# A decoder layer in one kernel: order of the expert's splits and scaling, column tiles for the gate product, a later wait for a low part

## What is computed

```python
# 1 attention, 16 heads of 32, chunks of 128 tokens
q, k, v = silu(x @ Wq), silu(x @ Wk), x @ Wv        # q, k rotated
o = lightning_attention(q, k, v)                    # decayed scores in a chunk, a state between chunks
o = rmsnorm_per_head(o * sigmoid(x @ Wg1 @ Wg2)) * norm_weight
x = layernorm(x + o @ Wo)                           # Wg1 is 512x32, Wg2 is 32x512
# 2 four experts chosen by token id, weights ctx
x = layernorm(x + expert_by_token_id(x))
# 3 48 experts, top 8 of each token, at most 192 tokens for an expert
g, u = split(xb[e] @ gate_up[e].T)                  # 192x512 @ 512x384
y[e] = (silu(g) * u) @ down[e].T                    # 192x192 @ 192x512
x = layernorm(x + sum of y, weighted)
```

## Time and profile before

| | |
|---|---|
| median of 3 runs | 951.74 us (949.85 to 955.11) |
| profiled execution, its own time | 962.05 us |
| span from first to last instruction | 960.2 us |
| PE busy | 856.5 us (89%) |
| DVE, ACT, POOL busy | 637.9, 397.1, 473.4 us |
| mean granted TensorE clock | 0.961 |

### The profile page before, as it was taken

How to read it: one execution, slowest core, us unless ns; L and a number is a source line. 1 busy time by engine, 2 the same in 40 slices (tenths; PEclk the granted TensorE clock), 3 DMA queues, 4 the chain that set the end, 5 groups by cost and what they waited for, 6 DMA issues and landing times. The chain is left out here.

```text
span 960.2 us, 18373 instructions
## 1 busy us (share of the span) xinstructions
PE 856.5 (89%) x5878; PEld 729.9 (76%) x5879; DVE 637.9 (66%) x1454; ACT 397.1 (41%) x805; POOL 473.4 (49%) x443
## 2 busy tenths in 40 slices
PE   6899999999999889999998699999999999999700
PEld 4787788778887668888887498888888888888600
DVE  6767765676567556777777667676776667666426
ACT  4333233222332412233322046666666665666504
POOL 0242333233433322555555357777776777775344
PEclk9899999999999999999999899999999999999955
DMA  9541112111210035322222849999999999997665
GB/s 331 189 167 45 45 45 87 44 44 44 86 45 33 23 109 167 105 101 99 94 93 99 288 127 287 265 274 280 268 271 268 280 275 261 287 236 164 164 168 215
DMA packets 72461, 155.39 MB, mean 162 GB/s; under 512 B 9872, under 2 KB 10304, under 8 KB 72032
## 3 DMA queue, kind: packets, MB, share of 16 engines
q1 hardware_dynamic: 49840, 99.40, 31.5%
q0 software_dynamic: 22576, 55.42, 23.8%
HBM read 110.27 MB, written 44.52 MB: 161 GB/s over the span
## 5 line engine op out<-in xcount | busy, mean ns | idle before, releaser
L1884 POOL DMA_INDIRECT y_rows<-arena,place_token x96 | 154.9, 1614 | 91.1 <-issue 72.0
L1873 POOL DMA_INDIRECT xg<-x_rows,place_token x96 | 103.5, 1078 | 43.0 <-issue 26.8
L940 PE MATMUL ps<-arena,raw 128*128 128x192 f32 x576 | 100.9, 333 | 1.2 <-DVE arena L1662 0.9
L940 PEld LDWEIGHTS ps<-arena,raw 128*128 128x128 f32 x576 | 95.9, 194 | 4.9 <-issue 4.2
L589 PE MATMUL ps<-w_hi,x_hi 128*128 128x512 f32 (+1 forms) x332 | 79.2, 361 | 4.6 <-DVE x_lo L1396 3.8
L940 PE MATMUL ps<-arena,mid_flat 128*128 128x192 f32 x432 | 74.7, 330 | 2.3 <-DVE arena L1662 2.3
L940 PEld LDWEIGHTS ps<-arena,mid_flat 128*128 128x128 f32 x432 | 69.9, 190 | 8.8 <-DVE arena L1662 8.5
L589 PE MATMUL ps<-w_lo,x_hi 128*128 128x512 f32 (+1 forms) x332 | 74.3, 346 | 0.0
L589 PE MATMUL ps<-w_hi,x_lo 128*128 128x512 f32 (+1 forms) x332 | 74.2, 346 | 0.0
L1745 POOL TENSOR_TENSOR arena<-arena,attn_pack 128x512 f32<-128x512 f32 x12 | 16.8, 1403 | 116.0 <-DVE arena L1287 116.0
L1146 ACT ACTIVATE arena<-ps,arena 96x512 f32<-96x512 f32 x48 | 32.8, 683 | 97.7 <-PE ps L953 94.8
(11 more groups left out here) (231 smaller groups left out, 1971.7 us busy)
## 6 DMA issues: line engine op xcount, KB each, us to landing
raw<-in_gu SPq DMA_DIRECT2D x24, 768.0 KB
mid_flat<-in_gu SPq DMA_DIRECT2D x18, 768.0 KB
raw<-in_dn SPq DMA_DIRECT2D x24, 256.0 KB
y_rows<-zero SPq DMA_DIRECT2D x20, 256.0 KB
mid_flat<-in_dn SPq DMA_DIRECT2D x18, 256.0 KB
arena<-in_gu SPq DMA_DIRECT2D x6, 768.0 KB
arena<-in_xT SPq DMA_DIRECT2D x16, 256.0 KB
x_res<-in_x SPq DMA_DIRECT2D x16, 256.0 KB, 2.7
```

What stands on the lines that cost most here:

```text
L940: m = pe.matmul(out, wgu[slot][:, q, part * P:(part + 1) * P], xgT[:, p, q, :], start=(q == 0), stop=(q == KC - 1))
L1873: pool.indirect_dma_start(out=xg[:, place, h, :], out_offset=None, in_=x2_d, in_offset=bass.IndirectOffsetOnAxis(ap=place_token[:, 2 * n + ...
L1884: pool.indirect_dma_start(out=y2_d if p and n < DUAL else y_d, out_offset=bass.IndirectOffsetOnAxis(ap=place_token[:, 2 * n + h:2 * n + h ...
```

## The change

Stage A: Wg1 is held once; `gate_low` becomes four separate products, one for each k, whose results lie in four column positions (partitions 0 to 31, 32 to 63 and so on), not summed. ACT's copy of them is plain float32 with 128 rows, and `gate_high` is four float32 products over 128 rows with Wg2 stacked four times, which does the sum. `low_g1`, `wg2_parts` and their two preparing instructions go. `project_o` starts on `o_high` and waits for the low part at its third pass. On DVE `low_o` moves behind the cut of the state's addition.

Stage C: on ACT the split of n's down weights comes first in turn n and `scale_y(n-1)` last; on DVE likewise: down weights' low part, h, `copy_x`, h's low part, `scale_y(n-1)`, `keep_w`. Scatter 42 no longer waits for scatter 41.

```diff
@@ ATTN_PACK
-             ("dq", P, (G, P)), ("block", P, (P,)), ("wg1", P, (KC, 3 * RANK))]
+             ("dq", P, (G, P)), ("block", P, (P,)), ("wg1", P, (KC, RANK))]
@@ tensor: gate_low, project_o, gate_high
-                    m = pe.matmul(ps[0:3 * RANK, PM, 0:P], wg1[:, k, :], xT[:, c % 2, k, :], start=(k == 0), stop=(k == KC - 1))
+                    m = pe.matmul(ps[k * RANK:(k + 1) * RANK, PM, 0:P], wg1[:, k, :], xT[:, c % 2, k, :], start=True, stop=True, skip_group_check=True)
...
-                pe.wait_ge(oT_copied, t + 1)
+                pe.wait_ge(o_high, t + 1)
...
-                three_passes(ps[:, PM, :], o_hi, o_lo, w_hi[:, 3], w_lo[:, 3], between=between).then_inc(wo_made, 1)
+                three_passes(ps[:, PM, :], o_hi, o_lo, w_hi[:, 3], w_lo[:, 3], (oT_copied, t + 1), between).then_inc(wo_made, 1)
...
-                pe.wait_ge(g1_low, t + 1)
+                pe.wait_ge(g1_copied, t + 1)
                 for g in range(G):
-                    m = pe.matmul(ps[:, PM, g * P:(g + 1) * P], wg2_parts[:, g * P:(g + 1) * P], g1_parts[:, :], start=True, stop=True)
+                    m = pe.matmul(ps[:, PM, g * P:(g + 1) * P], wg2[:, g * P:(g + 1) * P], g1[:, :], start=True, stop=True)
@@ scalar: c_expert
+                act.wait_ge(*weights_of(slot, turn))
+                at_least(act, dn_made[p], k)
+                act.activation(wdn_hi[p][:, 0, :], wdn[slot], ACT.Copy)
+                act.activation(wdn_hi[p][0:P // 2, 1, :], wdn_rest[slot], ACT.Copy)
+                act.activation(wdn_hi[p][P // 2:P, 1, :], wdn_rest[slot], ACT.Copy).then_inc(dn_high, 1)
                 act.wait_ge(gu_made[p], k + 1)
...
                 if not last:
                     copy_x(1 - p, k + p)
-                if not first:
-                    scale_y(1 - p, k - (1 - p))
-
-                act.wait_ge(*weights_of(slot, turn))
...
                 act.activation(hc_hi[P // 2:P, p, :], h_c[P // 2:P, p, :], ACT.Copy).then_inc(h_high, 1)
+                if not first:
+                    scale_y(1 - p, k - (1 - p))
@@ vector: a_tile
                 mask(t)
-                if not first:
-                    low_o(*last_of(b, c))
                 if c < CH - 1:
...
                                       block_diag[:, :].unsqueeze(1).to_broadcast([P, G, P]), ALU.mult).then_inc(add_cut, 1)
+                if not first:
+                    low_o(*last_of(b, c))
+                if c < CH - 1:
                     dve.wait_ge(add_cut, n + 1)
@@ vector: c_expert
+                dve.wait_ge(dn_high, 2 * k + p + 1)
+                dve.tensor_tensor(wdn_lo[p][:, 0, :], wdn[slot], wdn_hi[p][:, 0, :].bitcast(F32), ALU.subtract)
+                dve.tensor_tensor(wdn_lo[p][LO, 1, :], wdn_rest[slot], wdn_hi[p][rest_rows[slot], 1, :].bitcast(F32), ALU.subtract)\
+                   .then_inc(dn_split[p], 1)
                 dve.wait_ge(g_made, 2 * (2 * k + p) + 1)
...
                 if not last:
                     copy_x(1 - p, k + p)
+                dve.wait_ge(h_high, 2 * k + p + 1)
+                dve.tensor_tensor(ha_lo[:, p, :], h_a[:, p, :], ha_hi[:, p, :].bitcast(F32), ALU.subtract)
+                dve.tensor_tensor(hc[HI, p, :], h_c[HI, p, :], hc_hi[HI, p, :].bitcast(F32), ALU.subtract).then_inc(h_split, 1)
                 if not first:
                     scale_y(1 - p, k - (1 - p))
...
@@ gpsimd: c_scatter
-                if n >= DUAL:
+                if n > DUAL:
                     pool.wait_ge(y_added[1 - p], 32 * (k + p))
```

More of the change, by code:

```diff
@@ L205, in build @@
         weighted = take("weighted", [P, H, P])
-        wg2 = take("wg2", [3 * RANK, D]); wg2_parts = sb("wg2_parts", [3 * RANK, D], F32R)
-        g1_parts = sb("g1_parts", [3 * RANK, P], F32R)
+        wg2 = sb("wg2", [KC * RANK, D])
+        g1 = take("g1", [KC * RANK, P])
         tanh_gate = take("tanh_gate", [P, G, P])
@@ L359, in build @@
         ms_plus = sem("ms_plus"); rms_made = sem("rms_made"); o_normed = sem("o_normed")
-        r_spread = sem("r_spread"); r_turned = sem("r_turned"); wg2_high = sem("wg2_high"); wg2_split = sem("wg2_split"); g1_low = sem("g1_low"); oT_copied = sem("oT_copied"); wo_made = sem("wo_made")
+        r_spread = sem("r_spread"); r_turned = sem("r_turned"); oT_copied = sem("oT_copied"); wo_made = sem("wo_made")
         r1_made = sem("r1_made"); stat_made = sem("stat_made"); mv_made = sem("mv_made")
@@ L481, in _ @@
             sp.dma_start(xT[:, 1], d["xT"][1]).then_inc(xT_in[1], 16)
-            for i in range(3):
+            for i in range(KC):
                 sp.dma_start(wg2[i * RANK:(i + 1) * RANK, :], d["wg2"]).then_inc(late_in, 16)
@@ L490, in _ @@
             sp.dma_start(o2n_i[:, :], d["o2n"]).then_inc(gate_in, 16)
-            sp.wait_ge(late_in, 80)
+            sp.wait_ge(late_in, 16 * (KC + 2))
             sp.dma_start(token_of_slot_d.rearrange("(p j) a -> p (j a)", p=P), spare_i[:, :]).then_inc(slots_cleared, 16)
@@ L713, in a_tile @@
                 if first:
-                    pe.wait_ge(wg2_split, 1)
+                    pe.wait_ge(late_in, 16 * (KC + 2))
                 gate_high(t)
@@ L991, in copy_g1 @@
                 act.wait_ge(g1_made, t + 1)
-                act.activation(g1_parts[:, :], ps[0:3 * RANK, PM, 0:P], ACT.Copy).then_inc(g1_copied, 1)
+                act.activation(g1[:, :], ps[:, PM, 0:P], ACT.Copy).then_inc(g1_copied, 1)
             def copy_k(t):
@@ L1068, in _ @@
             high_x(0, 1)
-            act.wait_ge(late_in, 80)
-            act.activation(wg2_parts[:, :], wg2[:, :], ACT.Copy).then_inc(wg2_high, 1)
             tiles_of_a(act, a_tile, CH - 1)
@@ L1293, in plus_eps @@
                 dve.tensor_scalar(ms_eps[:, :], ps[:, PS, 0:H], 1.0 / HD, 4 * RMS_EPS, ALU.mult, ALU.add).then_inc(ms_plus, 1)
[L1295 to L1299, removed]
             def norm_o(b, c):
@@ L1357, in a_tile @@
                     plus_eps(*last_of(b, c))
-                low_g1(b, c)
                 if first:
@@ L1424, in _ @@
             rotated_sum(0, 0, 1)
[L1425 to L1428, removed]
+            dve.wait_ge(late_in, 16 * (KC + 2))
             tiles_of_a(dve, a_tile, CH - 1)
@@ L1688, in c_expert @@
                     keep_w(n + 1, 1 - p, k + p, (slot + 1) % 4)
[L1690 to L1696, removed]
             dve.wait_ge(y_seeded[0], 16 * (SLOT_T - SLOT_T // 2))
@@ L1942 @@
         "wo": rows(a["L0_attn_Wo"]),
-        "wg1": np.tile(rows(a["L0_attn_Wg1"]), (1, 1, 3)),
+        "wg1": rows(a["L0_attn_Wg1"]),
         "wg2": a["L0_attn_Wg2"],
```

## The result

The kernel after takes 937.03 us as the median of 4 runs (935.9 to 939.94), the kernel before 952.37 us beside it (949.85 to 955.11): the ratio is 0.9843, with a 95% interval of 0.9805 to 0.9881. The forecast was 936.2 us, in a range of 931 to 945. The kernel is faster by 15.3 us.

The account below looks back on a forecast made before the run. PE was taken to set the pace in stages A and C, the scatters' chain leading to the end. Stage C -11.5 and stage A -4 made -15.5 us; 951.74 - 15.5 = 936.2 us, range 931 to 945.

Parts of the forecast that it names:

- rival 2: Stage C: only the named waits go, the rest being PE's own sequencer; C gives 5.8, total 944 us; chance 0.09.
- all waits gone: 12.1 us, some tenths will be left: Stage C, turns 1 to 43: 2.3 us of waits in each of 5.24 groups of eight turns go; taken as -11.5 us.
- It waits for ACT's split of the down weights: Stage C: why DVE is late with h and `copy_x`; idle 1.39 us ahead of L1691.
- h can start as soon as silu allows, in all turns: Stage C, DVE: subtractions end by 4.35 us after `c_up` even with a table piece, the first silu at 4.4 us.
- Rival 4: Stage C: `scale_y` waits for scatter n-2's landing, margin 4 us; later landings lengthen every turn, 956 us or more; chance 0.03.
- Rival 1: Stage C: DMA sets the pace at 274 GB/s, so C gains nothing and the kernel takes 948 us; chance 0.06.
- Rival 3: Stage A: column positions cost in and out, A gives 0, total -11.5, 940 us; chance counted within the forecast's 0.78.
- the term of 0: Stage A, the gate's two products together: between -0.33 and +0.24 us a tile, taken as 0, bounds 0 and +4 us.
- by the row at most 0.13: Stage A, `gate_low`: saving a tile in column positions, with L697's idle times of 0.37 and 0.20 us counted.
- For c = 3 the term: Stage A: `project_o` no longer waits for the low part of o, -0.35 us in each of three tiles.
- a gain up to `c_down(42)` arrives at the end whole: The end: the scatters' chain from 43 on stays as long when it starts earlier; gains behind `c_down(42)` are lost.
- y2's load and scatter 42's dropped wait: The end: y2's earlier 4 MB load only shifts traffic, 0 with -2 to +2 us; the dropped wait costed at nothing.

Follow-up runs that it names:

- set 1: Runs of the kernel before (959.96 us), stage A's edits alone (ratio 0.998), stage C's edits alone (0.9864) and the unchanged kernel after (0.984).
- The two halves: Stage C's edits against the kernel before: split first with scaling in its old place, ratio 0.9896; scaling last with split in its old place, 0.9902.
- The kernel after of set 1: The kernel after again, no edit, against the kernel before: ratio 0.984 (0.9825 to 0.9856).
- stage C alone: Kernel before with only stage C's edits (order on ACT and DVE, scatter 42's dropped wait): ratio 0.9864 (0.9846 to 0.9882).
- sets 1 and 3: Set 1 has its own line; set 3 tested the end, with changes to y2's load and the pack of constants, ratios 0.9797 to 0.9838.
- the larger pack: Kernel after with Wg1 still held three times in the pack of constants, only the first copy read: ratio 0.9838 to the kernel before.
- the spread load: Kernel after with y2's four 1 MB pieces started one after the landing of scatters 42, 43, 44 and 45 each: 934.52 us, ratio 0.9797.
- sets 2 to 4: Set 2: parts of the stages, ratios 0.9896 to 0.9998; set 3: the end, 0.9797 to 0.9838; set 4: one more step there, 0.9769.
- the scaling-last kernel: Kernel before with stage C's edits, but the down weights' split in its old place behind `copy_x`; old stage A: ratio 0.9902 (0.9879 to 0.9924).

## Why the prediction was right, and where it was not

**The sum** (-15.5 us, measured -15.3 and -15.6) was right with two terms off in opposite directions: stage C gave 13.7 us for 11.5, more than its bound of 12.5, and stage A 2.2 for 4. The mechanism of stage C was right; that the sum met the measured time within 1 us is luck. (The chances of the cases add up to 0.91 for faster and 0.06 for same; 0.92 and 0.05 were written.)

**Stage C, the waits.** The two kinds were read rightly: the waits for the copy of x (1.1 us in eight turns) and the nameless ones for the low part of h (1.2 us) both went, the group fell by 2.55 us for 2.3, and rival 2 (the nameless ones are PE's own) is refuted by the 56.17 us. The term "all waits gone: 12.1 us, some tenths will be left" was 11.8 to 12.3 by the traces of before and after and those of set 1. The rest of the 13.7 us came from scatter 42 to 47, 1.4 us that were costed at 0. Whether they come from scatter 42's dropped wait is not shown: every kernel with an edit of stage C has that edit too.

**Stage C, why DVE was late.** "It waits for ACT's split of the down weights" was true and only half the cause. The two halves run alone show that ACT's scaling, which waits for `c_down(n-1)`, was in front of everything, and that either move takes the rest out from behind it. The step "h can start as soon as silu allows, in all turns" held, with the longest table piece too (0.03 us behind the silu); in the 42 turns it failed only in the two behind the wait for a landing, by 0.9 and 0.8 us.

**Rival 4, the landings.** The mechanism is real and small: one wait of 2.7 us in 42 turns, which cost 0.5 us. The margin of 4 us, taken from landings at the end, held in all other turns of this trace. The kernel after of set 1 has two such waits of ACT (2.6 us), stage C alone one of 0.5 us, and the five other kernels with the scaling last have none.

**Rival 1, DMA.** The rate rose to 290 GB/s and nobody waits for weights. Refuted.

**Rival 3, the column positions.** Their ways in and out cost 0.10 and 0.20 us, not 0.37 and 0.20, and in the ordinary tile the two products together gave nothing, as in the term of 0. The prediction's "by the row at most 0.13" for `gate_low` was too low a cap: it gave 0.39.

**Stage A, the sizes.** For c = 3 the term was -0.35 us and measured -0.65: I took the idle column (0.41) less some tenths, where start to start gives 0.57. For c = 1 and 2 it was -0.2 and measured -0.2 to -0.3, for c = 0 -0.1 and about -0.1. The gate's products were 0 and measured +0.02 us a tile. The first tile gave 1.25 and 1.65 us (sets 1 and 3), where 1 was taken for the first and last together. From the first `gate_low` to the last, set 1 shows 285.5 us for 291.3, so 5.9 us for the 4.

**Stage A, what arrives.** This is the step that failed: "a gain up to `c_down(42)` arrives at the end whole". Stage A's edits bring turn 1 4.9 us forward, and 1.7 us of it is lost between scatters 42 and 47. It goes with the gate's edits at least from scatter 43 to 44: 10.16 to 10.44 us in all five traces that have the gate's edits and the load unspread, 9.39 to 9.80 in the six without them. That link is only 0.7 of the 1.7 us; scatter 42 to 43 takes another 0.7 (12.25 and 11.54), and there kernels with and without the gate's edits mix (11.34 to 12.25 and 10.44 to 11.97). The pack's size is excluded; the fourth transfer of Wg2 and the changed buffers were not tried, so the cause stays open. The chain itself I had read in the earlier trace rows and left as it was: the 5.76 us ahead of scatter 43 against 3.50 ahead of 47 stood there, and asking what differs would have led to y2's load, and to 4 us more.

**y2's load and scatter 42's dropped wait** were costed at 0, with -2 to +2. From scatter 42 to 47 the chain took 41.76 us before and 41.59 after; between the kernels of one set the differences of -1.4 to +1.7 us stay in these bounds.

## What to carry to other kernels

When two engines share a turn, put what waits for the other engine's latest result last, and look at what stands behind each wait, not only at what it waits for. A serial chain of transfers at the end is a stage of its own: compare its links with each other, and where one is longer, look for the bulk load beside it and start that in steps. Read a nameless wait of PE from start to start, since its idle column starts at a modelled end (here 0.41 for 0.57 us), and compare traces only with ones of the same set of runs.

## What the runs showed of the hardware that was not expected

A bulk load of 4 MB beside an indirect scatter of 384 KB stretches the scatter's link from 6.6-6.9 to 9.4-12.3 us; the DMA rows below are of the kernel with the larger pack (four pieces at once) and of the one with the spread load, from 855 to 870 us: 317 and 213 GB/s.

```profile
855.00:870.00 15.00, 15.00 (x93) 13.26 (x92) 9.66 (x21) 10.43 (x24) 5.97 (x5) 1.00 1.04 317
```

```profile
855.00:870.00 15.00, 15.00 (x92) 13.44 (x91) 9.58 (x21) 9.82 (x22) 7.59 (x6) 1.00 0.77 213
```

One part of the level of a set of runs has a place. In every trace of set 1, and in that of before, DVE's mask starts 1.6 to 1.7 us behind `score` in seven of the eight tiles with c = 1 and 2; in every trace of sets 2 to 4, and in that of after, 1.24 us behind in these tiles, whatever the kernel. Here such a tile in the kernel before (set 1), then in the scaling-last kernel with the same stage A (set 2):

```profile
203.25 1.17 PE L688 MATMUL ps<-arena 32*128 32x128 f32 x32
203.36 0.69 DVE L1306 TENSOR_TENSOR arena<-ps,arena 128x512 f32<-128x512 f32 x1 [3.71 <-PE ps L635]
...
204.91 2.48 DVE L1341 TENSOR_TENSOR arena<-ps,arena 128x512 f32<-128x512 f32 x4 [0.85 <-PE ps L688]
```

```profile
202.22 1.17 PE L688 MATMUL ps<-arena 32*128 32x128 f32 x32
202.32 0.69 DVE L1305 TENSOR_TENSOR arena<-ps,arena 128x512 f32<-128x512 f32 x1 [3.71 <-PE ps L635]
...
203.46 2.48 DVE L1340 TENSOR_TENSOR arena<-ps,arena 128x512 f32<-128x512 f32 x4 [0.44 <-PE ps L688]
```

PE's rows ahead of it keep the same distances to 0.01 us; only the end of `score` reaches DVE 0.42 us later. It makes stage A 2.7 us longer (270.07 and 267.38 us from tile 1 to 15), and it is a quarter of the time by which the trace of before stood above that kernel's median. Stage B differed too (243.5 to 249.3 us from the last tile's `gate_low` to turn 1, over all traces), with no place found for it. Why the signal is late in one set and not in another stays open; sets 1 and 4 ran on the same chip, so it is not the chip alone.
